# Turning the heads' outputs: fp32 products with the identity, or fp16 halves and transposing transfers

## What is computed

```python
h = _layernorm(x)
q, k, v = (einsum('bsd,hde->bhse', h, W) for W in (Wq, Wk, Wv))
attn = softmax(where(causal, q @ k.T / 8, -inf))
heads = (attn @ v).transpose(0, 2, 1, 3).reshape(B, S, H * E)
y = _norm(h + heads @ Wo) * gamma + beta
x = x + y
x = x + moe(_layernorm(x))
```

## Time and profile before

| | us |
|---|---|
| median of 3 runs | 1676.04 |
| lowest, highest | 1673.46, 1676.71 |
| the profiled execution | 1674.17 |
| its span | 1672.4 |

### The profile page before, as it was taken

One profiled execution on the slowest core, in us unless ns is written; L12 is line 12 of the kernel. 1 busy time (PEld: TensorE's weight loads), 2 busy tenths in 40 slices (PEclk: granted clock), 3 DMA queues, 4 the chain that ended last, 5 costly groups with the idle time before them and its releaser, 6 DMA issues.

```text
span 1672.4 us, 56372 instructions
## 1 busy us (share of the span) xinstructions
PE 1601.0 (96%) x21209; PEld 1102.9 (66%) x21209; DVE 1414.9 (85%) x4461; ACT 1399.7 (84%) x2371; POOL 1410.6 (84%) x1183
## 2 busy tenths in 40 slices
PE   4799999999999999999999999999999999999968
PEld 1476776767667676676767667676776767666645
DVE  7889789898888989889898988989888898888645
ACT  3999898888989888888988989888898888888742
POOL 0687998979899797998979899797989979799874
PEclk8999999999999999999999999999999999999989
DMA  8655656556554564646446454654645456354523
GB/s 244 153 132 120 147 116 166 136 123 159 128 145 125 137 163 110 167 99 155 132 128 168 118 152 111 157 145 117 163 117 153 131 128 161 88 133 117 133 83 109
DMA packets 213902, 228.55 MB, mean 137 GB/s; under 512 B 20480, under 2 KB 178432, under 8 KB 213376
## 3 DMA queue, kind: packets, MB, share of 16 engines
q1 hardware_dynamic: 213632, 224.94, 52.5%
HBM read 84.89 MB, written 5.24 MB: 54 GB/s over the span
## 4 chain that ended last, share of the span: by engine, by line
PE 76%; POOL 8%; ACT 7%; issue 4%; DVE 2%; DMA 2%; SPq 0%; ACTq 0%; DVEq 0%; POOLq 0%
PE bank_r L393 19%; PE bank_s L393 15%; PE bank_u L393 12%; PE bank_x L393 10%; PE bank_v L393 9%; PE bank_g L393 7%; POOL p_lo L1484 3%; POOL expert_room L1499 2%; ACT p_hi L785 1%; POOL halves L1508 1%; ACT bank_x L804 1%; DMA expert_room<-comb_rows 1%; ACT y L804 1%; PE bank_g L402 1%; PE bank_v L402 1%
## 5 line engine op out<-in xcount | busy, mean ns | idle before, releaser
L1484 POOL TENSOR_TENSOR p_lo<-p,p_hi 128x1280 f16<-128x1280 f32 x256 | 671.3, 2625 | 135.6 <-ACT p_hi L785 135.1
L852 ACT ACTIVATE p<-bank_s,back 128x512 f32<-128x512 f32 (+1 forms) x768 | 462.6, 615 | 72.5 <-PE bank_s L393 53.4
L393 PE MATMUL bank_s<-score_ops 128*128 128x62 f16 (+10 forms) x4096 | 409.1, 232 | 3.7 <-ACT p L852 2.1
L393 PEld LDWEIGHTS bank_s<-score_ops 128*128 128x128 f16 x4096 | 285.2, 97 | 167.5 <-ACT p L852 19.0
L785 ACT ACTIVATE p_hi<-p 128x1280 f16<-128x1280 f32 x256 | 324.7, 1269 | 4.2 <-PE bank_r L393 1.7
L1499 POOL TENSOR_TENSOR expert_room<-expert_room 128x512 f32<-128x512 f32 x240 | 305.4, 1276 | 12.2 <-DMA expert_room<-comb_rows 10.4
L1508 POOL TENSOR_TENSOR halves<-expert_room,halves 128x512 f16<-128x512 f32 x240 | 277.7, 1164 | 0.5
L1127 DVE CUSTOM_DVE_ANT_0 max_junk<-bank_r,mask 128x384 f16<-128x384 f32 (+3 forms) x414 | 188.8, 489 | 18.8 <-PE bank_u L393 9.4
L393 PE MATMUL bank_x<-w_hi,halves 128*128 128x128 f16 x1920 | 197.7, 219 | 4.4 <-POOL halves L1508 4.3
L785 ACT ACTIVATE halves<-expert_room 128x512 f16<-128x512 f32 x240 | 151.0, 630 | 51.1 <-POOL expert_room L1499 34.2
L393 PE MATMUL bank_x<-w_lo,halves 128*128 128x128 f16 x960 | 172.3, 219 | 0.0
(11 more groups left out here) (282 smaller groups left out, 5009.9 us busy)
## 6 DMA issues: line engine op xcount, KB each, us to landing
score_ops<-nat SPq DMA_DIRECT2D x256, 256.0 KB, 3.9
score_ops<-nat SPq DMA_DIRECT2D x512, 128.0 KB, 3.8
expert_room<-comb_rows SPq DMA_DIRECT2D x240, 256.0 KB, 3.4
xt<-in_x SPq DMA_DIRECT2D x16, 256.0 KB, 3.4
xb<-in_x SPq DMA_DIRECT2D x16, 256.0 KB, 3.2
out_y<-expert_room SPq DMA_DIRECT2D x16, 256.0 KB, 3.8
score_ops<-comb_rows SPq DMA_DIRECT2D x16, 256.0 KB, 4.7
expert_room<-in_gate_up SPq DMA_DIRECT2D x1, 2048.0 KB, 10.1
```

Of the source, the lines that this page charges most:

```text
L393: return pe.matmul(dst, lhsT, rhs, start=start, stop=stop, skip_group_check=shared)
L852: act.activation(p32[:, h % P_SLOTS, at:at + cols], bank[score_bank(h, u)][:, 0:cols], ACT.Exp, scale=back[:, SC_SCORE:SC_SCORE + 1]).then ...
L1484: pool.tensor_tensor(p_lo[:, slot, :], p32[:, slot, :], p_hi[:, slot, :], ALU.subtract).then_inc(p_lo_done, 1)
```

## The change

Two halves are made before the turn instead of after it: `split_high` (ScalarE) copies `o32` to fp16, `split_low` (VectorE) subtracts that copy from `o32`; both go to a new tile `o_split`, which has one place. `turn_out` (SyncE) then issues one transfer with `transpose=True` of all 128 x 1024 fp16 elements into `oT`, in place of the four fp32 transposes. `times_wo` waits for the landing of two such transfers, `split_high` for that of the pair before. `rden` gets four places instead of two. To make room, `ex` shares the memory of `shifted` and `comb` that of `dropped`, and `mark_chosen` takes over a wait of `weigh`. All five engines' lists are written anew, with other banks. No other work is added or taken away. The diff, cut to the functions and, of the new loops, the parts the prediction speaks of:

```diff
...
-        rden = sb("rden", [P, 2, C], F32)
+        rden = sb("rden", [P, 4, C], F32)
         o32 = sb("o32", [P, 2, C, 2 * E], F32)
+        o_split = sb("o_split", [P, 2, C, 2 * E], F16)
         oT = sb("oT", [P, 2, 2, S], F16)
...
-        logits, dropped, shifted, ex = (
-            sb(name, [P, C, NE], F32) for name in ("logits", "dropped", "shifted", "ex"))
-        comb = sb("comb", [P, NE, C], F32)
+        logits, dropped, shifted = (
+            sb(name, [P, C, NE], F32) for name in ("logits", "dropped", "shifted"))
+        ex = shifted
+        comb = dropped[:, :, :].rearrange("p c e -> p (c e)").rearrange("p (e c) -> p e c", c=C)
...
-        oT_mm, oT_hi, oT_lo, y_mm, y0_done = sem("oT_mm"), sem("oT_hi"), sem("oT_lo"), sem("y_mm"), sem("y0_done")
+        o_hi_done, o_lo_done, y_mm, y0_done = sem("o_hi_done"), sem("o_lo_done"), sem("y_mm"), sem("y0_done")
+        oT_turned = [sem(f"oT_turned{k}") for k in range(2)]
...
+            def turn_out(m, q):
+                pair = m * PAIRS + q
+                sp.wait_ge(o_lo_done, pair + 1)
+                wait(sp, y_mm, m * QUADS + q // 2)
+                sp.dma_start(oT[:, q % 2].rearrange("p a (c t) -> p (a c) t", c=C), o_split[:, :, :, :].rearrange("p a c d -> p (a c d)"),
+                             transpose=True).then_inc(oT_turned[q % 2], 16)
...
+                place_max(n, 1); load_x(n + 2); spread_weights(n - 2, 15); turn_out(n, 0); place_qk(n, 5)
+                turn_out(n, 1); place_max(n, 2); turn_out(n, 2); store(n - 2); load_xb(n); place_qk(n, 6)
+                turn_out(n, 3); keep_weights(n - 1); spread_weights(n - 1, 0); spread_weights(n - 1, 1)
+                spread_weights(n - 1, 2); place_qk(n, 7); spread_weights(n - 1, 3); spread_weights(n - 1, 4)
+                place_max(n, 3); spread_weights(n - 1, 5); turn_out(n, 4); spread_weights(n - 1, 6); place_qk(n + 1, 0)
+                spread_weights(n - 1, 7); turn_out(n, 5); place_qk(n + 1, 1); place_qk(n + 1, 2); place_max(n + 1, 0)
+                spread_weights(n - 1, 8); spread_weights(n - 1, 9); spread_weights(n - 1, 10); turn_out(n, 6)
+                place_qk(n + 1, 3); turn_out(n, 7); spread_weights(n - 1, 11); spread_weights(n - 1, 12)
+                spread_weights(n - 1, 13); place_qk(n + 1, 4); spread_weights(n - 1, 14)
...
                 last.then_inc(pv_mm, 1)
 
-            def turn_heads(m, q, b):
-                take(b, oT_lo, m * PAIRS + q + 1)
-                pe.wait_ge(o32_done, m * H + 2 * q + 2)
-                turn32(bank[b], o32[:, q % 2]).then_inc(oT_mm, 1)
-
             def times_wo(m, g, b):
                 take(b, y0_done, m * QUADS + g + 1)
-                pe.wait_ge(oT_lo, m * PAIRS + 2 * g + 2)
+                for k in range(2):
+                    pe.wait_ge(oT_turned[k], 16 * (m * QUADS + g + 1))
...
+                times_v(n, 9, V); project(n + 1, 2, R0); values(n + 1, 1, R1); gate_product(n - 1, 4, G)
+                up_product(n - 1, 4, V); turn_maxima(n, 3, U); values(n + 1, 2, R0); down_product(n - 1, 0)
+                gate_product(n - 1, 5, U); project(n + 1, 3, G); max_scores(n + 1, 0, 1, R0, R1); down_product(n - 1, 1)
+                up_product(n - 1, 5, V); gate_product(n - 1, 6, R0); scores(n, 12, 0); times_v(n, 10, U)
+                values(n + 1, 3, R1); gate_product(n - 1, 7, R0); scores(n, 12, 1); scores(n, 12, 2); times_v(n, 11, V)
+                up_product(n - 1, 6, U); scores(n, 13, 0); scores(n, 13, 1); project(n + 1, 4, R0)
+                max_scores(n + 1, 0, 2, R1, U); down_product(n - 1, 2); down_product(n - 1, 3); scores(n, 13, 2)
+                max_scores(n + 1, 0, 3, R1, G); max_scores(n + 1, 0, 4, V, R0); scores(n, 14, 0)
+                up_product(n - 1, 7, U); project(n + 1, 5, R1); scores(n, 14, 1); times_v(n, 12, G); scores(n, 14, 2)
+                gate_product(n - 1, 8, R0); times_wo(n, 2, V); scores(n, 15, 0); times_v(n, 13, R1); scores(n, 15, 1)
+                max_scores(n + 1, 1, 0, U, R0); max_scores(n + 1, 1, 1, V, G); turn_maxima(n + 1, 0, R1)
+                down_product(n - 1, 4); down_product(n - 1, 5); scores(n, 15, 2); project(n + 1, 6, U)
+                gate_product(n - 1, 9, R1); up_product(n - 1, 8, V); project(n + 1, 7, R0); down_product(n - 1, 6)
+                up_product(n - 1, 9, U); down_product(n - 1, 7); max_scores(n + 1, 1, 2, R0, G); scores(n + 1, 0, 0)
+                scores(n + 1, 0, 1); gate_product(n - 1, 10, R1); scores(n + 1, 0, 2); max_scores(n + 1, 1, 3, G, V)
+                times_v(n, 14, R0); times_v(n, 15, U); up_product(n - 1, 10, G); scores(n + 1, 1, 0)
+                project(n + 1, 8, V); scores(n + 1, 1, 1); max_scores(n + 1, 1, 4, R0, G); down_product(n - 1, 8)
+                gate_product(n - 1, 11, U); scores(n + 1, 1, 2); project(n + 1, 9, R0); times_v(n + 1, 0, R1)
+                down_product(n - 1, 9); gate_product(n - 1, 12, G); up_product(n - 1, 11, V); times_wo(n, 3, U)
+                scores(n + 1, 2, 0); turn_maxima(n + 1, 1, R0); down_product(n - 1, 10)
...
                 copy(p_hi[:, slot, :], p32[:, slot, :]).then_inc(p_hi_done, 1)
 
-            def o_high(m, q, b):
-                act.wait_ge(oT_mm, m * PAIRS + q + 1)
-                wait(act, y_mm, m * QUADS + q // 2)
-                copy(oT[:, q % 2, 0, :], bank[b][:, :]).then_inc(oT_hi, 1)
+            def split_high(m, q):
+                pair = m * PAIRS + q
+                act.wait_ge(o32_done, m * H + 2 * q + 2)
+                wait(act, oT_turned[(pair - 1) % 2], 16 * ((pair + 1) // 2))
+                copy(o_split[:, 0].rearrange("p c d -> p (c d)"), o32[:, q % 2].rearrange("p c d -> p (c d)")).then_inc(o_hi_done, 1)
...
+                copy_maxima(n, 2, R1); exps(n, 7, 2); residual_apply(n - 1); p_high(n, 7); split_high(n, 2)
+                v_high(n, 7, R0); qk_high(n, 14, R1); exps(n, 8, 0); qk_high(n, 15, U); exps(n, 8, 1); exps(n, 8, 2)
+                h_high(n + 1, R0); second_apply(n - 1); split_high(n, 3); h2_high(n - 1); p_high(n, 8)
+                qk_high(n + 1, 0, U); exps(n, 9, 0); exps(n, 9, 1); gate_tanh(n - 1, 0, R1); exps(n, 9, 2)
+                v_high(n + 1, 0, R0); route(n - 1); exps(n, 10, 0); gate_tanh(n - 1, 1, G); p_high(n, 9)
...
 
             def denominators(m, h, b):
                 dve.wait_ge(pv_mm, m * H + h + 1)
-                dve.reciprocal(rden[:, h % 2, :].rearrange("p (c a) -> p c a", a=1), pv_bank(b)[:, :, E:E + 1]).then_inc(rden_done, 1)
+                dve.reciprocal(rden[:, h % 4, :].rearrange("p (c a) -> p c a", a=1), pv_bank(b)[:, :, E:E + 1]).then_inc(rden_done, 1)
 
             def divide(m, h, b):
                 q, ab = h // 2, h % 2
                 dve.wait_ge(rden_done, m * H + h + 1)
                 if ab == 0:
-                    wait(dve, oT_mm, m * PAIRS + q - 1)
+                    wait(dve, o_lo_done, m * PAIRS + q - 1)
                 dve.tensor_tensor(o32[:, q % 2, :, E * ab:E * ab + E], pv_bank(b)[:, :, 0:E],
-                                  rden[:, h % 2, :].rearrange("p (c a) -> p c a", a=1).to_broadcast([P, C, E]), ALU.mult).then_inc(o32_done, 1)
-
-            def o_low(m, q, b):
-                dve.wait_ge(oT_hi, m * PAIRS + q + 1)
-                dve.tensor_tensor(oT[:, q % 2, 1, :], bank[b][:, :], oT[:, q % 2, 0, :], ALU.subtract).then_inc(oT_lo, 1)
+                                  rden[:, h % 4, :].rearrange("p (c a) -> p c a", a=1).to_broadcast([P, C, E]), ALU.mult).then_inc(o32_done, 1)
+
+            def split_low(m, q):
+                dve.wait_ge(o_hi_done, m * PAIRS + q + 1)
+                dve.tensor_tensor(o_split[:, 1], o32[:, q % 2], o_split[:, 0], ALU.subtract).then_inc(o_lo_done, 1)
 
...
             def mark_chosen(p):
                 wait(dve, drop_done, C * p)
+                wait(dve, combT_mm, p)
...
-                wait(dve, combT_mm, p)
...
+                divide(n, 11, V); times_up(n - 1, 6, U); split_low(n, 5); row_maximum(n + 1, 0, 2, 0, R1)
+                qk_low(n + 1, 4, R0); row_maximum(n + 1, 0, 2, 1, U); row_maximum(n + 1, 0, 3, 0, R1)
+                row_maximum(n + 1, 0, 3, 1, G); row_maximum(n + 1, 0, 4, 0, V); row_maximum(n + 1, 0, 4, 1, R0)
+                denominators(n, 12, G); qk_low(n + 1, 5, R1); times_up(n - 1, 7, U); gate_times_tanh(n - 1, 8, R0)
+                add_heads(n, 2, V); divide(n, 12, G); denominators(n, 13, R1); divide(n, 13, R1)
+                row_maximum(n + 1, 1, 0, 0, U); row_maximum(n + 1, 1, 0, 1, R0); row_maximum(n + 1, 1, 1, 0, V)
+                split_low(n, 6); row_maximum(n + 1, 1, 1, 1, G); qk_low(n + 1, 6, U); times_up(n - 1, 8, V)
+                qk_low(n + 1, 7, R0); gate_times_tanh(n - 1, 9, R1); row_maximum(n + 1, 1, 2, 0, R0)
+                row_maximum(n + 1, 1, 2, 1, G); times_up(n - 1, 9, U); row_maximum(n + 1, 1, 3, 0, G)
+                gate_times_tanh(n - 1, 10, R1); row_maximum(n + 1, 1, 3, 1, V); denominators(n, 14, R0)
```

(5 more changed lines are left out.)

1089 lines of the change are left out of this document (520 added, 569 removed).

## The result

| | before | after |
|---|---|---|
| median | 1676.38 | 1739.21 |
| lowest, highest | 1673.46, 1676.87 | 1735.6, 1740.28 |
| span of the profiled execution | 1672.4 | 1738.5 |

The change makes the kernel slower: the ratio is 1.0375, with an interval of 1.0356 to 1.0394. I had forecast 1642 us, faster.

A forecast was written before the change was run, and what follows sets the result against it. TensorE's own list was taken to pace the loop. From 1674.2 us, 49.3 for removed transposes went off, 12 taken back and 3 for the tail came on: 1639.9, plus 1.9 to the median, 1642 us; range 1620 to 1695.

The forecast's parts named there:

- What is removed: TensorE's fp32 transposes of the heads' outputs: 0.44 us a call, 3.5 us a lap, 49.3 us over batches 0 to 13.
- the tail: Last batch: the turn before the fourth times_wo takes 5.2 us instead of 3.0, not hidden: +3 us (0 to 8).
- less a quarter: Share of the gain taken back by queues and by other engines 90 to 92% busy: 12 us, 0.9 a lap.
- Rival 2: The transposing transfer is slow, gain eaten at 6.4 us to landing, 1706 us at 7.5; chance 0.18.
- What is exchanged: split_high replaces ScalarE's o_high, split_low VectorE's o_low, 128 each: split_low 0.64 us against 0.69, so no change if alone.
- rival 1: split_low with two SBUF operands and GpSimd's instructions hold each other up: some 1668 us; chance 0.25.
- the formula: Mean wait of a split_low coming at any moment, from the lengths of GpSimd's three large instructions: 0.74 us.
- My own upper bound: GpSimd held by split_low and keeping all 9.2 us of its p_hi waits: a lap of 103 us, 1731 us in the end.
- (a): End of times_v(n, 15) to times_wo(n, 3): 7.5 us of TensorE work against 6.2 for the way round, 1.3 left.
- (b): To times_wo(n, 2): 8.4 us of TensorE work against 6.5 for the way round, 1.9 left.
- (c): On ScalarE split_high(n, 3) comes some 5.9 us after split_high(n, 2); 4.6 is needed, 1.3 left.
- Rival 3: The ring of all engines paces the loop, TensorE's freed 3.5 us turn into waits: about 1679 or 1676 us; chance 0.12.

The follow-up runs named there:

- run 1: The changed kernel with split_low reading one SBUF operand, so a second copy of the high half replaces the low half: 1654.4 us, ratio 0.9875.
- run 2: The kernel before with o_low reading two SBUF operands (a constant tile in place of the bank): 1729.99 us, ratio 1.0327.
- run 5: The changed kernel with split_low issued as two instructions of 128x256 in place of one of 128x512: 1839.44 us.
- run 6: The changed kernel with GpSimd's p_low issued as two instructions of 128x640 in place of one of 128x1280: 1717.89 us.
- Run 7: The kernel of run 1 with an extra VectorE instruction before each split_low, 1680.19 us; with GpSimd's p_low in two instructions, 1670.39; with both, 1685.71.
- run 8: The kernel of run 1 with four extra VectorE instructions in a row before every fourth split_low: 1718.44 us (pairs 0 and 4), 1731.23 (3 and 7).

## Why the prediction was wrong

*What bounds the kernel.* Right: TensorE paced before, and once the collision is gone it is 98.8% busy at a lap of 97.4 us (run 1).

*What is removed, added, and the tail.* The forecast's mechanism is right where the collision is away, its sizes a little too good. A lap lost 2.2 us (99.6 to 97.4); I had 3.5 less a quarter, 2.6. The first batches gained nothing: the third store is 3.4 us later in run 1 than before, where I had counted 0.44 us for each of their turns and called that generous. From the fourteenth store (1437.5 in run 1; in the kernel before 1458.0, the row below) to the end it takes 1650.9 - 1437.5 = 213.4 us there and 1672.4 - 1458.0 = 214.4 before: the 3 us of the tail are not seen.

```profile
L332 SPq DMA_DIRECT2D comb_rows<-expert_room x12: 344/344/347, 363.1 to 1458.0; - x12
```
Together 1654 instead of 1642.

*The transfer.* I took 3.9 us to landing; it is 3.4 in the middle and 5.7 at most, the issue 1.26 us within my 0.69 to 1.77. Rival 2 is out: TensorE waits 1.6 us for it in 1000, and among ScalarE's waits there is none for it. The Trainium skill, Advanced Engine Details and Errata (X-Bar Transpose), has transposing transfers as fast as regular ones: here 3.4 us against 2.4 for the same bytes, not quite equal, but far from the 10.5 us that the prediction estimated from the Trainium skill's other page.

*What is exchanged: the step that failed.* "No change, as long as it runs alone", a term of nothing, with rival 1 at a chance of 0.25 and 1668 us. It measured 84.8 us (after against run 1). The mechanism was named. Two things were wrong.

First the chance: the kernel before had no large VectorE instruction of the loop with two SBUF operands, and I read this as "nothing shows what it costs" when GpSimd, 89% busy with instructions of up to 2.6 us, made the condition of the rule certain. The rule is that of the Trainium skill, SBUF — State Buffer (Who interferes with whom): an exclusive lock, held for the whole instruction, between a VectorE instruction with two SBUF inputs and a GpSimd one that reads SBUF. Runs 1, 2, 5 and 6 agree with it: no wait with one SBUF operand (653 to 687 ns), a wait to the end of the running instruction (0.55 us behind it), and one as long for half the columns.

Second the price, 26 us over my forecast for 84.8. The mean wait was sized well, 0.74 us by the formula and 1.473 - 0.680 = 0.79 measured, but partly by luck: the formula lets `split_low` come "at any moment", and in the trace each of the eight waits of a lap has its own length, from none to 2.0 us, nearly the same in lap after lap. GpSimd is held less than forecast, 39.5 / 16 = 2.5 us a batch for 5.4. And I set the means, 5.9 us a lap for VectorE and 5.4 for GpSimd, against the slack of the engines, with half of GpSimd's waits kept. My own upper bound, all waits kept, was a lap of 103 and 1731 us (14 laps at 3.5 us and 3 for the tail on 1676 would be 1728), and the lap is 102.8. That is luck: the bound is 88.5 of work, 5.4 of holding and 9.2 of waits for `p_hi`, and the lap has 0.891 x 102.8 = 91.6 of GpSimd's work with the holding, 7.2 of those waits (69.6 in 1000), and 4.0 of others, which the bound doesn't have.

Run 7 shows that busy times alone give 31 to 49 us. What the runs show in their place is the single wait: TensorE stands still for `v_lo` once a lap, 2.1 us behind a `split_low` that waits 2.0, and the clock falls behind it in seven of nine laps; run 8 gets 38 to 51 us from lumps of that length alone. That this and GpSimd's part are all of the rest stays argued. The covers I had worked out for (a), (b) and (c) are 1.3, 1.9 and 1.3 us. I had the numbers for this and didn't hold the spread against the covers, nor name who stands behind `split_low` on VectorE: the statistics of the norms and `v_lo`. Of the clock the prediction says nothing.

*Rival 3* is no part of it: in run 1 TensorE waits 12 us in 1000.
